# A two-layer adaLN / Mamba-2 / FFN kernel: two of the next unit's x tiles are made in a unit's first part, a gate product opens the unit, and VectorE makes a tile's products ahead of the next masks

## The reference, cut to what matters

```python
h = layernorm(x) * (1 + ca) + sa
proj = einsum('bsd,ed->bse', h, in_proj_w)          # gate 8192, x 8192, B 1024, C 1024, dt 128
hBC = silu(causal depthwise conv of 4 taps(x, B, C) + conv_b)
dt = clip(softplus(dt + dt_bias), 0, 100); A_dt = -exp(A_log) * dt
# 128 heads of 64, 8 groups of 16 heads, chunks of 128 tokens
Y_diag = einsum('bzlhn,bzshn,bhzls,bzshp->bzlhp', C, B, exp(segsum(A_dt)), x * dt)
Y_off  = C . (state carried from chunk to chunk) * exp(cumsum(A_dt))
y = Y_diag + Y_off + x * D
g = y * silu(gate);  g = g * rsqrt(mean over the group of g*g + eps) * norm_w
x = x + ga * (g @ out_proj_w);  then layernorm, sign(weight) product, bias, residual
```

## Time and profile before

| | |
|---|---|
| median of 3 runs | 1873.5 us (1872.71 to 1877.07) |
| profiled execution: its time | 1870.32 us |
| its span, first to last instruction | 1868.5 us |
| PE busy (matmuls) | 1754.7 us, 94% |
| DVE, ACT, POOL busy | 1290.5, 1065.5, 942.1 us (69%, 57%, 50%) |
| mean granted TensorE clock | 0.988 |

### The profile page before, as it was taken

The page is one execution under the profiler, slowest core; times in us unless marked ns, Lnnn a source line. Parts: engine busy times, 40 slices in busy tenths (PEclk is TensorE's granted clock), DMA queues, the critical chain, the costliest instruction groups (busy, mean ns, idle before and its releaser), DMA issues.

```text
span 1868.5 us, 31134 instructions
## 1 busy us (share of the span) xinstructions
PE 1754.7 (94%) x9656; PEld 1344.0 (72%) x9656; DVE 1290.5 (69%) x2095; ACT 1065.5 (57%) x1946; POOL 942.1 (50%) x721
## 2 busy tenths in 40 slices
PE   6799999999999999999999999999999999999966
PEld 5567777777777777777777777777777777777755
DVE  5766667666766677766676667666777666766788
ACT  6566555656646565665546566465656555565632
POOL 2355453556535464554535555355644545455563
PEclk9899999999999999999999999999999999999988
DMA  6412121111202121121211212121211212111121
GB/s 224 130 30 69 55 66 44 50 60 57 66 28 72 49 66 51 35 66 55 66 45 48 62 54 68 29 72 45 70 51 29 72 55 66 44 48 61 34 96 57
DMA packets 77097, 114.14 MB, mean 61 GB/s; under 512 B 21376, under 2 KB 28032, under 8 KB 76032
## 3 DMA queue, kind: packets, MB, share of 16 engines
q1 hardware_dynamic: 59360, 80.06, 14.2%
q10 hardware_dynamic: 17568, 31.99, 5.1%
HBM read 88.94 MB, written 23.07 MB: 60 GB/s over the span
## 4 chain that ended last, share of the span: by engine, by line
issue 46%; POOL 34%; PE 9%; DVE 5%; ACT 3%; DMA 1%; SPq 1%; POOLq 1%; ACTq 0%; DVEq 0%
POOL yt L1605 9%; POOL ssq L1600 7%; POOL wg_lo L1524 4%; POOL wo_lo L1524 4%; POOL prev L1586 3%; POOL yt L1608 3%; POOL wx_lo L1524 3%; PE bank L476 2%; PE bank L478 2%; PE bank L477 2%; PE bank L641 1%; PE bank L706 1%; DMA raw_w<-w_in_dram 1%; PE bank L840 1%; ACT lm L1072 0%
## 5 line engine op out<-in xcount | busy, mean ns | idle before, releaser
L1605 POOL TENSOR_TENSOR yt<-yt,ea 128x384 f32<-128x384 f32 (+1 forms) x128 | 189.6, 1481 | 393.1 <-DVE ea L1440 393.1
L1218 DVE SCALAR_TENSOR_TENSOR xc<-bank,bpar,xc 128x511 f32<-128x511 f32 (+2 forms) x384 | 285.4, 743 | 52.8 <-ACT xc L906 48.3
L1410 DVE TENSOR_TENSOR lm<-lm,cbm 128x512 f32<-128x512 f32 x256 | 185.9, 767 | 155.7 <-ACT lm L1075 155.7
L476 PE MATMUL bank<-h_hi,wg_hi 128*128 128x512 f32 x640 | 262.0, 409 | 31.3 <-ACT gate L1030 21.9
L478 PE MATMUL bank<-h_hi,wg_lo 128*128 128x512 f32 x640 | 251.0, 392 | 0.0
L477 PE MATMUL bank<-h_lo,wg_hi 128*128 128x512 f32 x640 | 250.2, 391 | 0.0
L476 PE MATMUL bank<-wo_hi,g_hi 128*128 128x512 f32 x496 | 206.9, 417 | 7.2 <-POOL wo_lo L1524 7.2
L476 PE MATMUL bank<-h_hi,wx_hi 128*128 128x512 f32 x512 | 210.3, 411 | 2.2 <-DVE bt L1218 2.2
L1586 POOL TENSOR_TENSOR prev<-prev,dec 128x512 f32<-128x512 f32 x96 | 102.0, 1063 | 206.0 <-DVE prev L1356 131.9
L478 PE MATMUL bank<-h_hi,wx_lo 128*128 128x512 f32 x512 | 200.3, 391 | 0.0
L477 PE MATMUL bank<-h_lo,wx_hi 128*128 128x512 f32 x512 | 199.9, 390 | 0.0
(11 more groups left out here) (187 smaller groups left out, 3796.9 us busy)
## 6 DMA issues: line engine op xcount, KB each, us to landing
raw_w<-w_in_dram SPq DMA_DIRECT2D x145, 256.0 KB, 2.6
raw_w<-w_out_dram SPq DMA_DIRECT2D x64, 256.0 KB, 2.6
part_d<-part ACTq DMA_DIRECT2D x64, 256.0 KB, 2.0
part<-part_d ACTq DMA_DIRECT2D x58, 256.0 KB, 2.7
rt<-rows_d SPq DMA_DIRECT2D x256, 8.0 KB
acc<-x_dram SPq DMA_DIRECT2D x8, 256.0 KB, 6.6
acc<-w_mod_dram SPq DMA_DIRECT2D x2, 1024.0 KB, 6.0
lh<-neg_d SPq DMA_DIRECT2D x128, 8.0 KB
```

What stands on the lines that cost most here:

```text
L476: nc.tensor.matmul(out_ap, whi(k), hhi(k), start=(k == 0), stop=False)
L1218: stt(dst[:, at], ps[:, 0:HALF - 3 + k], w(k), dst[:, at], ALU.mult, ALU.add)\
L1410: tt(lm[:, h % 4, :], lm[:, h % 4, :], cbm[:, toks(hf)], ALU.mult).then_inc(v_m, 1)
L1605: tt(yt[:, j % 2, cols], yt[:, j % 2, cols], ea[:, j % 2, cols], ALU.add).then_inc(p_t3, 1)
```

## The change

It moves work between a unit's two parts and reorders DVE and ACT. In detail:

- The x tiles of the next unit are made in the order 2, 3, 0, 1 (`X_ORDER`). Tiles 2 and 3 are made in the first part, after `transposes(2)` and `transposes(3)`; tiles 0 and 1 behind the diagonal products of j = 0 and 1 (in c = 3: j = 2 and 3, behind the B and C products). `xc` gets two more slots, so tiles 2 and 3 alternate between two places.
- First part on PE: `gate 1, transposes 0, transposes 1, gate 2, out 0, states 0, transposes 2, x 2, out 1, states 1, transposes 3, x 3, gate 3, out 2, states 2, exp_a 0, diff 0, diff 1, out 3`. Before: `gate 1, gate 2, transposes 0, out 0, transposes 1, out 1, states 0, transposes 2, gate 3, states 1, transposes 3, out 2, states 2, exp_a 0, diff 0, diff 1, out 3`.
- The fourth output product goes to bank 1 (`out_bank`); gates use banks 0 and 1 (and 7 for tile 0 in c = 0).
- DVE in the j loop: t2 and t1 of tile j, then the two masks of tile j + 1, then `lower_g(j - 1)`, then the conv. `lower_g(3)` moves into the next unit, behind the first two `scale_x`.
- ACT: decays before the copy ea; two weight splits at the unit's opening, the taps and silu of tiles 2 and 3 in the first part.
- POOL: the fills of the unit's first step come ahead of the state's decay; the B and C weights come behind those of tiles 2 and 3. `prev` has one slot less.

```diff
-        xc = sb("xc", [128, NCT, HALF])
+        xc = sb("xc", [128, NCT + 2, HALF])
-        prev = sb("prev", [128, NZ + 1, BLOCK])
+        prev = sb("prev", [128, NZ, BLOCK])
...
+        X_ORDER = (2, 3, 0, 1)
+        def xslot(hf, j):
+            return j if j < 2 else j + 2 * hf
...
         def by_step(todo):
             if len(todo) == 6:
-                return [todo[0:1], todo[1:3], todo[3:4], todo[4:6]]
-            return [todo[z:z + 1] for z in range(4)]
+                return [todo[0:2], todo[2:3], todo[3:5], todo[5:6]]
+            return [todo[0:2], todo[2:3], todo[3:4], []]
...
+        def out_bank(z):
+            return 1 if z == 3 else None
...
+                if z == 0 and c == 0:
+                    te.wait_ge(v_bcconv, 4 * (g + 1))
+                    te.wait_ge(v_conv, 4 * u + 2)
+                elif z == 0:
+                    te.wait_ge(a_ea, 4 * (u - 1) + 1)
+                elif z == 1:
+                    te.wait_ge(v_conv, 4 * u + (3 if c == 0 else 4))
...
+                else:
+                    te.wait_ge(v_conv, 4 * (u + 1) + 1)
...
+                def next_x(j):
+                    if hf == 1:
+                        te.wait_ge(p_w, filled(g, x_fill(c, j)))
+                    if j == 2:
+                        te.wait_ge(a_gate, 4 * u + 2)
+                    elif j == 3:
+                        te.wait_ge(a_gate, 4 * u + 3)
+                    elif c == 3:
+                        te.wait_ge(v_bcconv, 4 * (g + 1) + 2 + j)
+                    elif j == 0:
+                        te.wait_ge(v_prev, sb0 + (3 if hf else 4))
+                    elif first:
+                        te.wait_ge(a_gate, 4 * (u + 1))
+                    else:
+                        out_read(g, c, 3)
+                    project(("x", j), x_bank(c, j), hv)
...
+                def next_work(j):
+                    if c == 3:
+                        if j < 2:
+                            next_bc(2 * j)
+                            next_bc(2 * j + 1)
+                        else:
+                            next_x(j - 2)
+                    elif j < 2:
+                        next_x(j)
+                    elif j == 2:
+                        gate_proj(g, c + 1, 0)
...
+                transposes(0)
+                transposes(1)
                 gate_proj(g, c, 2)
+                previous(0)
+                states(0)
+                transposes(2)
+                next_x(2)
+                previous(1)
+                states(1)
+                transposes(3)
+                next_x(3)
+                gate_proj(g, c, 3)
+                previous(2)
+                states(2)
+                exp_a(0)
+                diff(0)
+                diff(1)
+                previous(3)
...
-                exp_a(0)
                 decays(0)
+                exp_a(0)
...
+                scale_x(0)
+                scale_x(1)
+                if not first:
+                    lower_g(u - 1, (c - 1) % UPG, NCT - 1)
+                    group_sums(u, g1, b1, h1)
+                new_state(0)
+                scale_x(2)
+                previous(0)
+                next_conv(("x", 2))
+                previous(1)
+                new_state(1)
+                scale_x(3)
+                next_conv(("x", 3))
...
                 for j in range(NCT):
...
+                    if j < NCT - 1:
+                        mix(2 * j + 2)
+                        mix(2 * j + 3)
                     if j >= 1:
-                        lower_g(j - 1)
+                        lower_g(u, c, j - 1)
```

More of the change, by code:

```diff
@@ L705, in transposes, with previous @@
                     for j in range(NCT):
[L706 removed]
+                        lst = nc.tensor.transpose(bank[2 + z % 2][:, j * 128:(j + 1) * 128], xc[:, xslot(hf, j), chunk(z)],
                                                   ident[:, :])
                     lst.then_inc(t_xt, 1)
+                def previous(z):
+                    if first or (end and z > 0):
+                        return
+                    if z == 0 and hf == 1:
+                        te.wait_ge(p_w, filled(g, 3 if c == 1 else 15))
+                    if z == 3:
+                        te.wait_ge(a_gate, 4 * (u + 1))
+                    out_proj(u - 1, z, out_bank(z), (g, c))
+                    if z == 0:
+                        if c == 0:
+                            te.wait_ge(v_bl, 2 * g + 1)
+                        if c in (0, 3):
+                            sum_squares(g - 1 if c == 0 else g, 1 if c == 0 else 0)
@@ L784, in unit @@
                     if j == 0:
-                        if not end:
-                            ge(te, v_acc, 4 * u)
+                        if not end and not first:
+                            out_read(g, c, 1)
                     else:
@@ L1141, in unit @@
                 split_g(NCT - 1)
+                if more and c == 3:
+                    silu_x(u + 1, hv, 1)
             def group(g, last, first):
@@ L1367, in unit, with scale_x @@
                         vec.tensor_copy(bt[:, toks(h2)], bank[6 + h2][:, :]).then_inc(v_bl, 1)
-                for z in range(NZ):
+                def scale_x(z):
                     ve.wait_ge(t_xt, 4 * u + z + 1)
@@ L1392, in unit, with previous @@
-                    if end and z == 3:
-                        ve.wait_ge(a_bcsilu, 2 * GROUPS)
-                        for v in range(2):
-                            for k in range(NK):
-                                i = 16 + v * NK + k
-                                ts((ga_row, gb_row)[v][:, k * 128:(k + 1) * 128], ident[:, :], small[:, i:i + 1], None,
-                                   ALU.mult).then_inc(v_diag, 1)
-                items, n = proj_items(c, last), 0
+                def previous(z):
+                    if not first and not (end and z > 0):
+                        accumulate(u, g1, b1, h1, z, out_bank(z))
@@ L1402, in unit, with next_conv, lower_g @@
+                items = proj_items(c, last)
                 nv, hv = (nb, 1) if hf == 0 else (nb + 1, 0)
                 pv = (c // 2) if hf == 0 else (c // 2 + 1) % 2
+                def next_conv(item):
+                    if not end:
+                        conv(item, item_bank(c, item), nv, hv, g + 1, pv)
+                def lower_g(v, cv, j):
+                    ve.wait_ge(a_hi, 4 * v + j + 1)
+                    ghi, glo = g_parts(end and cv == c)
+                    if j == 0 and not (end and cv == c):
+                        ge(ve, t_out, 4 * v)
+                    stt(glo[:, j, :], yt[:, j % 2, :], par(cv // 2, j, NORM), ghi[:, j, :].bitcast(F),
+                        ALU.mult, ALU.subtract).then_inc(v_lo, 1)
@@ L1405, in mix @@
+                if end:
+                    ve.wait_ge(a_bcsilu, 2 * GROUPS)
+                    for v in range(2):
+                        for k in range(NK):
+                            i = 16 + v * NK + k
+                            ts((ga_row, gb_row)[v][:, k * 128:(k + 1) * 128], ident[:, :], small[:, i:i + 1], None,
+                               ALU.mult).then_inc(v_diag, 1)
                 def mix(h):
```

301 lines of the change are left out of this document (142 added, 159 removed).

## The result

The changed kernel takes 2023.8 us (median of four, 2022.6 to 2026.7); the kernel before, run beside it, 1873.1. The ratio is 1.0807, interval 1.0781 to 1.0833: slower by 8%, some 150 us, and far outside the predicted range. The direction was right, the size was not.

A forecast was written before the change was run, and what follows sets the result against it. PE sets the end, with POOL's chain setting the next unit's first output product in units 0 and 2. Eight groups' 30.4 us less 0.35 made 1870.3 into 1900.3; 3.2 to the median gave 1903, range 1850 to 1920.

The forecast's parts named there:

- POOL's chain: Units 0 and 2: from POOL's add of j = 2 to the next unit's first output product, 11.10 us.
- Contention: Two masks beside each POOL add of j below 3: 0 to 10 us over 24 chains, left out of the sum.
- The masks free 1.2 us: j = 0 and 1: masks moved behind DVE's products free about 1.2 us for POOL, included in the sum.
- Placement of the convs: Units 0 and 2: convs of x(0) and x(1) start 4.7 and 10.5 us after the first diagonal product's end.
- The wait at g(3) of unit 3: First part: the fourth gate product waits for bank 1, held by the conv of x(2): +1.15 us a group.
- The wait for acc: First part, unit 3: the 1.44 us accumulation wait, once a group, goes with the fourth output bank: -1.5 us.
- Waits for ea at the last tile of unit 3: Two products of j = 2 end about 21.2 us in, PE arrives at 19.2: a wait of 2.0 us.
- Units 0 and 2: First diagonal product's end to next unit's first output product takes 25.1 us, costing 2.1 and 1.0 us a group.
- Unit 1: First diagonal product's end to next unit's first output product takes 23.7 us against 23.0 allowed, costing 0.7 us.
- (d): Rival, slower still: masks hold POOL up (+10) and x weights come late in units 1 and 3; 1920 and up; chance 0.12.
- (b): Rival, faster: DVE keeps PE's pace, POOL's add of j = 2 starting before 12.5 us; 1835 to 1867; chance 0.24.
- (c): Rival, no change: moved work fits and POOL sets the first output product about as now; 1868 to 1879; chance 0.14.

The follow-up runs named there:

- e1: Changed kernel with DVE making the next tile's two masks ahead of the current tile's products, as before the change: 1946.6 us, ratio 1.0376.
- e4: Kernel before, with only the mask order changed: a tile's products ahead of the next masks; 1936.8 us, ratio 1.0327.
- e6: Changed kernel with POOL's add and gate product replaced by a four-column sum and one constant fill; 1880.4 us, ratio 1.0050.
- e9: Changed kernel with POOL's add and gate product replaced by a four-column sum and eight 64-column fills, nearer POOL's real time; 1889.6 us, ratio 1.0110.
- e2: Changed kernel with taps and convs of x(0) and x(1) one tile earlier in DVE's and ACT's lists (units 0 to 2); 1992.6 us, ratio 1.0620.
- e3: Changed kernel with both masks first and taps and convs of x(0) and x(1) one tile earlier; 1972.6 us, ratio 1.0516.
- e7: Kernel before, with only the fourth output product moved to a third bank; 1862.1 us, ratio 0.9949.
- e12: Changed kernel with masks first, plus twelve extra matmuls behind each of x(0) and x(1) in units 0 to 2; 2033.5 us, ratio 1.0872.
- e8: Changed kernel with gate product 1 of units 1 to 3 in bank 7, x(2) waiting for bank 1 instead; 1998.9 us, ratio 1.0684.

## Why the prediction was wrong

**What bounds the kernel, and POOL's chain: right, but hidden.** O was set by POOL's chain, and its 11.10 us were met with 11.05 in e1, with waits for wo_lo of 1.35 us on average where I had forecast 1 to 2. In the changed kernel this step doesn't show, since PE comes later still. POOL's add of j = 2 starts 13.7 us after E (366.46), 14.0 forecast. But POOL then pauses 1.08 us for the gate's silu on ACT (373.50), and its last wo_lo ends at 378.80, 12.3 us after that add; PE, held by gate product 1, starts O at 380.70. I had said that without a wait for wo_lo the chain would have been shorter than 11.1 us and PE free. Neither was so.

**Contention: the step that failed first.** "0 to 0.44 us more on each chain, 0 to 10 us", left out of the sum. The order that brings it costs 61 us in the old kernel (e4) and 81 in the new one (e1), and e6 and e9, with the order kept, show that POOL's reads are what makes it dear. The 0.44 was POOL's side of one overlap; DVE's side was not priced. On DVE the pair of masks gains 0.8 us (2.11 against 1.29) and the lower_g behind it 1.0 (1.76 against 0.74), in the busiest of the helpers, the one that PE waits for. Over the kernel that is 256 x 0.28 + 124 x 0.36 = 116 us of DVE by the mean ns, against 106 us more of DVE busy in all. The Trainium skill (SBUF — State Buffer, Who interferes with whom) says that DVE and GpSimd share a pair of ports under an exclusive lock. The trace agrees more closely than I had granted: the ends above are those of instructions that wait for each other by turns. POOL's add gains 0.37 us, about what the first mask still had to run (354.13 + 0.60 lies 0.43 us after the add's start), and masks fall to 694 ns when POOL's add and gate product don't read. I had that rule before me, set it at 10 us more, and counted it on POOL alone.

**The masks free 1.2 us: right for POOL, paid for on DVE.** POOL's add of j = 0 starts 1.57 us after E (354.30 - 352.73), 2.82 before (329.69 - 326.87). But it then runs beside the masks, and all that stands behind them on DVE, the conv last, comes later.

**Placement of the convs: misread.** The convs were put in DVE's list directly behind the tile that makes their product (starts at 4.7 and 10.5 after E). The list of items in the changed code is `[[], [x(0)], [x(1)], []]`: each stands a tile later. They started at 10.2 and 17.3, and x(1)'s conv holds the bank of gate product 1: 67.6 us of waits, of which 28.8 are left in e9 without POOL's reads. Yet the order is not an error that one could simply undo: e2 gives back 35 us, and with the masks first it costs 26 (e3).

**The wait at g(3) of unit 3: right in its doubt.** 1.15 us were priced; in the changed kernel it didn't wait for xc, in e1 it waited 0.66 us (group 2). The wait for acc went as forecast, and e7 shows it worth 10 us by itself.

**Waits for ea at the last tile of unit 3: right in place, wrong in size.** 2.0 us forecast; 3.9 in group 2, up to 4.0. Without POOL's reads (e9) they are 1.8 in seven waits, so the size was right for a kernel without the contention. In e1 they are 3.0, with masks of 1.28 us standing ahead of the products again.

**The clock: not in the prediction at all.** The earlier trace rows show 1.00, and a PE that waits 7 us in a turn, in short pieces; I took it as given that a wait costs its own length, and that only waits could move. PE's busy time grew by 67 us of the 150, as matmuls after the long waits ran at the lower level. A wait of 2.8 us cost some 4.4 (2.81 + 4.45 - 2.87).

**What is left of the sum.** With most of the contention gone, e1's stretches give 8 x (2.7 + 3.5 + 1.6) + 7 x 3.9 = 90, less 14 in the first parts: 76 against 70 measured. The part that I had worked out (30 us) was less than half of that. Units 0 and 2 came within 0.6 us of the forecast (25.7 for 25.1). Unit 1 was 2.8 us longer (26.5 for 23.7) and unit 3 by 3.7 (42.1 for 38.4). In e9, with the contention and 0.75 us of POOL's chain gone, unit 1 is 1.0 us over and unit 3 by 2.2, while units 0 and 2 are 0.7 under. So those two are the mis-sized terms, partly by late convs and partly by contention that I had left out.

**Rivals.** (d), slower still, was the nearest, but its mechanism was half right: masks and POOL hold each other up, for six to eight times the +10 given, and no x weight came late. (b) is excluded; its deciding point, POOL's add of j = 2 before 12.5 us after E, was missed at 13.7. (c) is excluded by the 2023.8.

**What stays open.** The 70 us of e1 are waits for ea, xc, wo_lo and g_lo, and 16 us of slower matmuls. How they divide isn't settled. Contention has a share still (masks of 895 ns against 767), the place of the convs has one, and so has the product of cover that left each tile. e12 shows that 38 us of the waits can be filled, not what makes them. The old kernel without POOL's reads, which would give the price of the placement alone, wasn't run, and orders with other pairs of tiles weren't tried.

## What to carry to other kernels

Before moving an elementwise operation on one of DVE and POOL, look up which instruction of the other it will then run beside, and price both sides; here the order that brought the two together cost 61 to 81 us of 1873. A product moved off a loop takes its cover with it: count what the slowest in-order engine needs per tile, not only PE. If mending one wait makes another of the same size (e8, e2), stop mending places and take load off the engine behind them; and try the parts of a change one by one: of the two tried alone here, the third bank gained 10 us and the masks' new order lost 61.

## What the runs showed of the hardware

- Two DVE masks of 128 x 512 with both inputs in SBUF took 1.29 us with POOL idle (in e1) and 1.28 beside its fills (in e6), and 2.11 beside POOL's two-input operations. Fills by POOL (MEMSET, 524 ns for 512 columns in e6) did not lengthen them: 693 ns a mask over the whole of e6 and 694 in e9, 767 before, 1049 after.
- A single lower_g took 1.76 us in place of 0.74 when it started 0.40 us into POOL's gate product, and ended 0.56 us after it; in e1 one that starts ahead of POOL's add takes 0.74, and the add 1.44 in place of 1.01. Who starts first keeps its time.
- After a PE wait of 2.81 us, with one of 1.07 us a microsecond ahead of it and a full stream before that, the granted clock was 0.54 over the next 3.75 us (0.43 us from matmul to matmul in place of 0.23), though it had been 1.00 up to the wait. In e1, where the same places have waits of 1.05 and 0.93 us (group 2), it stayed at 1.00. The mean granted clock was 0.950 in the changed kernel, 0.988 before; with useless matmuls in the wait it was 0.980, and the kernel was 0.8% faster with 4% more matmuls.
